# Turning both quantised activations by DMA in a fused attention and FP4 feed-forward kernel

## The reference

```python
x = layernorm(x + attn(x, W_write, W_read, decay, log_alpha))
x = layernorm(x + ffn(x, w_gate, w_up, w_down))

def fp4_quant_dequant(x):            # blocks of 16 along the last dimension
    scale = max(max(abs(xb)) / 6.0, 1e-12)
    xn = xb / scale
    q = GRID[searchsorted(MID, abs(xn))] * sign(xn) * scale   # GRID 0, .5, 1, 1.5, 2, 3, 4, 6
def fp4_linear(x, w):
    return einsum('bsk,nk->bsn', fp4_quant_dequant(x), fp4_quant_dequant(w))
gate = fp4_linear(x, w_gate)         # 256 -> 704
y = fp4_linear(x, w_up)              # 256 -> 704
h = silu(gate) * y
return fp4_linear(h, w_down)         # 704 -> 256
```

## Time and profile before

| | |
|---|---|
| time, median of 3 runs | 324.39 us (324.23 to 324.56) |
| span of the profiled execution | 322.5 us |
| TensorE busy | 314.5 us (97%) |
| VectorE busy | 293.0 us (91%) |
| GpSimd busy | 238.2 us (74%) |
| ScalarE busy | 213.2 us (66%) |
| DMA queue of SP | 15.01 MB, 14.0% of 16 engines |

### The profile page before, as it was taken

One profiled execution on the slowest core, in us unless ns is written; L12 is line 12 of the kernel. 1 busy time (PEld: TensorE's weight loads), 2 busy tenths in 40 slices (PEclk: granted clock), 3 DMA queues, 4 the chain that ended last, 5 costly groups with the idle time before them and its releaser, 6 DMA issues.

```text
span 322.5 us, 6519 instructions
## 1 busy us (share of the span) xinstructions
PE 314.5 (97%) x2067; PEld 285.2 (88%) x2067; DVE 293.0 (91%) x746; ACT 213.2 (66%) x521; POOL 238.2 (74%) x258
## 2 busy tenths in 40 slices
PE   7999999999999999999999999999999999999994
PEld 3999988989998998999989998898989889998983
DVE  4799789989899999899998999889999999999973
ACT  7769994767775647844784556766675555665664
POOL 1999898668696868676886768777779588368872
PEclk9999999999999999999999999999999999999999
DMA  6830301010010200320020200021000000001002
GB/s 227 302 125 9 132 0 67 1 66 2 1 67 16 84 16 0 100 82 3 16 83 17 83 17 3 33 65 35 1 18 17 16 18 17 19 16 35 17 33 84
DMA packets 8242, 15.69 MB, mean 49 GB/s; under 512 B 1040, under 2 KB 5136, under 8 KB 8208
## 3 DMA queue, kind: packets, MB, share of 16 engines
q1 hardware_dynamic: 7920, 15.01, 14.0%
q10 hardware_dynamic: 288, 0.26, 0.3%
HBM read 11.08 MB, written 4.19 MB: 47 GB/s over the span
## 4 chain that ended last, share of the span: by engine, by line
PE 69%; DVE 17%; issue 5%; ACT 4%; POOL 3%; ACTq 0%; DVEq 0%; POOLq 0%
PE gu L1712 11%; PE gu L1716 11%; PE gu L1713 11%; PE bank L1817 5%; PE bank L1712 4%; PE bank L1716 4%; PE bank L1713 4%; PE bank L1722 3%; DVE h_y L1094 3%; PE bank L1725 3%; PE bank L1726 3%; DVE w_raw L1209 2%; DVE hqT_lo L1236 2%; DVE h_am L1215 2%; PE bank L1783 2%
## 5 line engine op out<-in xcount | busy, mean ns | idle before, releaser
L413 POOL TENSOR_TENSOR h_q<-h_g,h_ns 128x704 f32<-128x704 f32 x32 | 51.2, 1604 | 47.7 <-DVE h_g L1099 47.6
L1712 PE MATMUL gu<-guT_hi,xqT_hi 128*128 128x512 f32 (+1 forms) x192 | 74.0, 386 | 0.7 <-DVE w_raw L1209 0.6
L1713 PE MATMUL gu<-guT_lo,xqT_hi 128*128 128x512 f32 (+1 forms) x192 | 72.2, 376 | 0.0
L1716 PE MATMUL gu<-guT_hi,xqT_lo 128*128 128x512 f32 (+1 forms) x192 | 56.6, 376 | 0.0
L699 ACT ACTIVATE w_raw<-gu 128x512 f32<-128x512 f32 x64 | 29.3, 462 | 32.7 <-PE gu L1716 32.4
L406 POOL TENSOR_TENSOR h_n<-w_raw,h_rs 128x704 f32<-128x704 f32 x32 | 47.0, 1472 | 3.4 <-DVE h_rs L1089 3.2
L719 ACT CAST hqT_hi<-bank 128x512 fp32r<-128x512 f32 x64 | 30.4, 478 | 17.7 <-PE bank L1817 17.2
L1712 PEld LDWEIGHTS gu<-guT_hi,xqT_hi 128*128 128x128 f32 x192 | 36.1, 188 | 6.0 <-ACT xqT_hi L688 0.9
L1716 PEld LDWEIGHTS gu<-guT_hi,xqT_lo 128*128 128x128 f32 x192 | 35.5, 188 | 6.0 <-ACT xqT_lo L693 0.2
L1713 PEld LDWEIGHTS gu<-guT_lo,xqT_hi 128*128 128x128 f32 x192 | 36.1, 188 | 4.8
L1094 DVE SCALAR_TENSOR_TENSOR h_y<-h_sq,h_n 128x704 f32<-128x704 bf16 x34 | 36.9, 1090 | 0.0
(11 more groups left out here) (159 smaller groups left out, 936.7 us busy)
## 6 DMA issues: line engine op xcount, KB each, us to landing
xs<-in_x_rows_dram SPq DMA_DIRECT2D x8, 512.0 KB, 3.4
out_dram<-wq_gu SPq DMA_DIRECT2D x32, 128.0 KB, 1.7
x_full<-in_xt_rows_dram SPq DMA_DIRECT2D x7, 512.0 KB, 3.2
w_raw<-in_w_ffn_dram SPq DMA_DIRECT2D x6, 352.0 KB, 6.0
w_pair<-in_w_attn_dram SPq DMA_DIRECT2D x1, 512.0 KB, 5.2
x_full<-in_xt_rows_dram SPq DMA_DIRECT2D x1, 256.0 KB, 2.6
x_full<-in_xt_rows_dram ACTq DMA_DIRECT2D x1, 256.0 KB, 3.4
scal<-in_scalars_dram ACTq DMA_DIRECT2D x1, 1.0 KB, 1.7
```

The source lines that it names most:

```text
L413: nc.gpsimd.tensor_tensor(blocks(h_q[:, p, 0:I]), blocks(h_g[:, p, :]), per_block(h_ns[:, p, :], HB), ALU.mult).then_inc(h_quant, 1)
L1712: nc.tensor.matmul(dst, lh, rh, start=(first and i == 0), stop=False)
L1713: nc.tensor.matmul(dst, lh, rl, start=False, stop=False)
L1716: last = nc.tensor.matmul(dst, ll, rh, start=False, stop=(end and i == len(terms) - 1))
```

## The change

For tiles 0 to 29 and for all x, TensorE no longer transposes activations. What is on the grid (x_g, h_g) becomes bf16, which holds its values exactly, and a DMA on SP transposes it (turn_x_grid, turn_h_grid) from SBUF to SBUF. The scales take another way: they are written in the order of the chunks into x_ns or h_ns, TensorE transposes them (one lone transpose per tile or half batch, x_scale_rows, h_scale_rows), ScalarE copies them to SBUF, SP writes them to DRAM and reads them back, each row 16 times (spread_x_scales, spread_h_scales). GpSimd multiplies the turned grid by the spread scales (x_spread, h_spread, now 768 wide), and ScalarE and VectorE split the product in one instruction each (h_round_all, h_rest_all), which read SBUF instead of PSUM. Tiles 30 and 31 keep the old way.

Beside it: all squares are written to PSUM in float32; the eight PSUM banks are one tensor with a place for every call given in tables; the subtractions of v and xq through the negated identity go; the negated mean of the output is folded into GpSimd's out_stats, except for the last tile; x_moments works on one column at a time; z_off shares the memory of dist. ScalarE issues the loads of x from batch 1 (rows) and 2 (transposed) on and all stores but the last; SP has the scale transfers and turns alone, behind the first loads. Before its first product gate_up waits for silu_ready, and for h_ready only before the second. All orders are new and written out without a loop. In TensorE's order gate_up(0) now stands ahead of reads(1, 1) and of everything of batch 2, down(4) behind gate_up(11), down(16) behind gate_up(23), down(24) behind gate_up(30, first half).

```diff
+        x_g = sb("x_g", [P, 2, PAIR], BF16)
+        x_gT = sb("x_gT", [P, 2, 2 * DK, P], BF16)
+        x_s = sb("x_s", [XHELD, 2, P])
+        x_sT = sb("x_sT", [P, 2, PAIR])
...
+        h_g = sb("h_g", [P, 2, HPAD], BF16)
+        h_gT = sb("h_gT", [P, 2, HC, P], BF16)
+        h_s = sb("h_s", [SHELD, 2, P])
+        h_sT = sb("h_sT", [P, 2, HPAD])
...
+        h_scales_dram = nc.dram_tensor("h_scales_dram", [B * TILES, SHELD, P], F32, kind="Internal").ap()
+        x_scales_dram = nc.dram_tensor("x_scales_dram", [2 * B, XHELD, P], F32, kind="Internal").ap()
...
+        def over_rows(rows, held, used):
+            return rows[0:KB * held, :].rearrange("(k c) t -> k (c t)", c=held)[:, 0:used * P].unsqueeze(1).to_broadcast((KB, BLK, used * P))
...
+            def write_h_scales(k, p, turn):
+                sp.wait_ge(hs_copied, k + 1)
+                sp.dma_start(h_scales_dram[k], h_s[:, p, :]).then_inc(hs_written[p], 16)
+            def spread_h_scales(k, p, turn):
+                sp.wait_ge(hs_written[p], 16 * turn)
+                if turn > 1:
+                    sp.wait_ge(h_quant, k - 1)
+                sp.dma_start(h_sT[:, p, :], over_rows(h_scales_dram[k], SC, HC)).then_inc(hs_landed[p], 16)
+            def turn_h_grid(k, p, turn):
+                sp.wait_ge(hg_repeated, k + 1)
+                if turn > 1:
+                    sp.wait_ge(h_quant, k - 1)
+                sp.dma_start_transpose(h_gT[:, p, :, :], h_g[:, p, :]).then_inc(hg_turned[p], 16)
...
+            write_h_scales(19, 1, 10)
+            spread_x_scales(6, 0)
+            spread_h_scales(19, 1, 10)
+            turn_h_grid(19, 1, 10)
+            write_h_scales(20, 0, 11)
+            turn_x_grid(6, 0)
+            turn_h_grid(20, 0, 11)
+            spread_h_scales(20, 0, 11)
...
+            def h_spread(k, p, turn):
+                pool.wait_ge(hs_landed[p], 16 * turn)
+                pool.wait_ge(hg_turned[p], 16 * turn)
+                if k >= 2:
+                    pool.wait_ge(hT_lo_ready, 2 * k - 2)
+                else:
+                    pool.wait_ge(wT_filled, FILLS)
+                nc.gpsimd.tensor_tensor(h_q[:, p, :], h_gT[:, p, :, :].rearrange("p c t -> p (c t)"), h_sT[:, p, :],
+                                        ALU.mult).then_inc(h_quant, 1)
...
-            def h_squares(k, p):
+            def h_squares(k, p, free):
                 act.wait_ge(h_norm, k + 1)
-                nc.scalar.activation(h_sq[:, p, :], h_n[:, p, :], ACT.Square, scale=ROOT_K).then_inc(h_square, 1)
+                wait_all(free)
+                nc.scalar.activation(two_banks(h_sq_at[k]), halves(h_n[:, p, :]), ACT.Square,
+                                     scale=ROOT_K).then_inc(h_square, 1)
...
+            def hg_repeat(k, p):
+                act.wait_ge(h_grid, k + 1)
+                nc.scalar.copy(h_g[:, p, I:HPAD], h_g[:, p, I - TAIL:I]).then_inc(hg_repeated, 1)
+            def repeat_h_scales(k, p):
+                act.wait_ge(h_div, k + 1)
+                ns = h_ns[:, p, 0:SROWS].rearrange("p (s e c) -> p c s e", s=2, c=SC)
+                nc.scalar.copy(ns[:, HC - 1, 1, :], ns[:, HC - 1, 0, :]).then_inc(hs_repeated, 1)
+            def copy_h_scales(k, p, turn):
+                act.wait_ge(hs_filled, k + 1)
+                if turn > 1:
+                    act.wait_ge(hs_written[p], 16 * turn - 16)
+                nc.scalar.copy(h_s[:, p, :], ps[0:SHELD, hs_at[k], 0:P]).then_inc(hs_copied, 1)
+            def h_round_all(k, p):
+                if k >= 2:
+                    act.wait_ge(down_filled, k - 1)
+                act.wait_ge(h_quant, k + 1)
+                nc.scalar.copy(hqT_hi[:, p, :], h_q[:, p, :]).then_inc(hT_hi_ready, 2)
...
+            def load_x_transposed(n):
+                act.wait_ge(xT_lo_ready, 2 * n)
+                act.dma_start(x_full[:].rearrange("p c t -> p (c t)"), xt_rows[n]).then_inc(xt_loaded, 16)
+            def store(k, slot):
+                act.wait_ge(out_ready, k + 1)
+                act.dma_start(out_rows[k], o_out[:, slot, :]).then_inc(stored[slot], 16)
...
+            def h_rest_all(k, p):
+                dve.wait_ge(hT_hi_ready, 2 * k + 2)
+                nc.vector.tensor_tensor(hqT_lo[:, p, :], h_q[:, p, :], hqT_hi[:, p, :].bitcast(F32),
+                                        ALU.subtract).then_inc(hT_lo_ready, 2)
...
+            def h_scale_rows(k, p, free):
+                pe.wait_ge(hs_repeated, k + 1)
+                wait_all(free)
+                nc.tensor.transpose(ps[0:SHELD, hs_at[k], 0:P], h_ns[:, p, :], ident[:]).then_inc(hs_filled, 1)
...
                 if k >= 1:
-                    pe.wait_ge(h_ready, 2 * k + half - 1)
+                    pe.wait_ge(h_ready if half else silu_ready, 2 * k + half - 1)
+                wait_all(free)
...
+                    if k >= 1 and m == 1:
+                        pe.wait_ge(h_ready, 2 * k - 1)
```

More of the change, by code:

```diff
@@ L1976, in _ @@
-            run(body)
-            down(12, 0, [(v_lo_ready, 13)])
-            values(6, 1, [(hT_lo_ready, 27)])
-            h_transpose(14, 2, 0, [(o_ready, 13)])
-            xq_transpose(4, 1, [(pr_ready, 27)])
+            h_scale_rows(3, 1, [(hs_copied, 3)])
+            reads(2, 1, [(wT_lo_ready, 8)])
+            x_scale_rows(2, 0, [(h_grid, 4)])
+            h_scale_rows(4, 0, [(h_grid, 4)])
+            gate_up(5, 1, 1, 1)
+            scores(3, 0, [(z_ready, 6)])
+            gate_up(6, 1, 2, 0)
@@ new lines, in _ @@
+            gate_up(8, 2, 0, 0)
+            down(1, 1, [(hs_copied, 7)])
+            scores(3, 2, [(v_lo_ready, 8)])
+            gate_up(8, 2, 0, 1)
+            scores(3, 3, [(pr_ready, 15)])
+            x_scale_rows(3, 0, [(o_ready, 2)])
+            h_scale_rows(7, 1, [(o_ready, 1)])
+            gate_up(9, 2, 1, 0)
+            reads(3, 1, [(h_grid, 8)])
+            gate_up(9, 2, 1, 1)
+            down(2, 2, [(z_ready, 8)])
+            down(3, 3, [(x_grid, 7)])
+            h_scale_rows(8, 0, [(pr_ready, 16)])
@@ new lines, in _ @@
+            gate_up(10, 2, 2, 0)
+            scores(4, 0, [(hs_copied, 9)])
+            scores(4, 1, [(h_grid, 9)])
+            values(4, 0, [(h_grid, 9)])
+            h_scale_rows(9, 1, [(pr_ready, 18)])
+            gate_up(10, 2, 2, 1)
+            gate_up(11, 2, 3, 0)
+            reads(4, 0, [(o_ready, 4)])
+            x_scale_rows(3, 1, [(pr_ready, 17)])
+            gate_up(11, 2, 3, 1)
+            down(4, 0, [(xs_copied, 8)])
+            down(5, 1, [(x_grid, 8)])
+            h_scale_rows(10, 0, [(z_ready, 9)])
@@ new lines, in _ @@
+            gate_up(12, 3, 0, 0)
+            values(4, 1, [(h_grid, 11)])
+            scores(4, 2, [(h_grid, 11)])
+            scores(4, 3, [(hs_copied, 11)])
+            h_scale_rows(11, 1, [(o_ready, 5)])
+            gate_up(12, 3, 0, 1)
+            gate_up(13, 3, 1, 0)
+            x_scale_rows(4, 0, [(hs_copied, 12)])
+            down(6, 2, [(pr_ready, 19)])
+            gate_up(13, 3, 1, 1)
+            reads(4, 1, [(h_grid, 12)])
+            down(7, 3, [(x_grid, 9)])
+            h_scale_rows(12, 0, [(z_ready, 10)])
@@ new lines, in _ @@
+            gate_up(14, 3, 2, 0)
+            scores(5, 0, [(o_ready, 7)])
+            scores(5, 1, [(o_ready, 8)])
+            values(5, 0, [(hs_copied, 13)])
+            h_scale_rows(13, 1, [(h_grid, 14)])
+            gate_up(14, 3, 2, 1)
+            gate_up(15, 3, 3, 0)
+            x_scale_rows(4, 1, [(hs_copied, 14)])
+            down(8, 0, [(pr_ready, 22)])
+            reads(5, 0, [(xs_copied, 10)])
+            gate_up(15, 3, 3, 1)
+            down(9, 1, [(o_ready, 9)])
+            gate_up(16, 4, 0, 0)
@@ L1982, in _ @@
+            values(5, 1, [(o_ready, 10)])
+            scores(5, 2, [(h_grid, 15)])
+            scores(5, 3, [(h_grid, 15)])
+            x_scale_rows(5, 0, [(z_ready, 11)])
+            h_scale_rows(14, 0, [(x_grid, 10)])
+            gate_up(16, 4, 0, 1)
+            gate_up(17, 4, 1, 0)
+            reads(5, 1, [(hs_copied, 15)])
+            scores(6, 0, [(h_grid, 16)])
+            h_scale_rows(15, 1, [(z_ready, 12)])
             gate_up(17, 4, 1, 1)
             gate_up(18, 4, 2, 0)
-            down(13, 1, [(pr_ready, 28)])
+            values(6, 0, [(xs_copied, 11)])
```

2554 lines of the change are left out of this document (1495 added, 1059 removed).

## The result

The changed kernel takes 334.37 us, the median of four runs (331.22 to 340.36), where the kernel before took 324.44 beside it: 1.027 times as long, 95% interval 1.025 to 1.030. Each median here is over all runs, while a ratio and its interval leave out disturbed runs, more than 1.5% above the fastest of their kernel (here 340.36). The prediction was 309, faster. The profiled execution took 333.26 us, its span is 331.5, and by the sum of the prediction it should have been 307.

What follows compares the result with a forecast made beforehand. TensorE was taken as the bound, VectorE 4% behind. TensorE's span of 322.5 less 22 is 300.5, plus 6 idle 306.5; with VectorE at 298 to 307, span 307 and median 309; forecast 303 to 314, full range 299 to 342.

Steps and rivals of the forecast that it cites:

- the one on the spread's engines: Spread of scales: 2.8 us, or 4.5 if 8 outer parts use half the engines; taken at 4, said not to matter.
- stands still for the landing of each write: SP waits 1.7 us for each write of scales to land, 78 us in all, within 265 us of tiles.
- 22 us less: TensorE's net saving: 28.3 us removed, 6.4 added for 46 lone scale transposes; 16 to 23 by the bounds.
- front gap: Start of TensorE's order, gate_up(0) waiting for a turn of x: 6 us idle charged, 0 to 12.
- 278 predicted: VectorE's busy time after 15 us less, 9 to 22; with idle time its span is 298 to 307.
- 138 issues at 0.33: SP's issues of scale writes, spreads and turns, 46 us; with 78 for landings, 124 us of some 265.
- The bound of 3.4 for a turn's issue: SP would bind only if issuing a turn took over 3.4 us, filling the 265 us in which tiles flow.
- turns bind: Rival: non-overlapping turns bind above 6.5 us per h turn; 340 us at 7; slower, chance 0.28.
- Its signs: Turns over 6.5 us would show as GpSimd's DMA waits ahead of its new product and TensorE below 90% mid-run.
- The block by block reading: Turn of h: 1309 ns per 128x128 block adds up, six make 7.9 us, time 375; 0.1 of the 0.28.
- Late but not binding: Rival: in-order engines lose part of the gain to late landings, front gap 12; 314 to 323 us, chance 0.15.
- pieces of one row each: Upper end for a 128x768 turn: 768 pieces of 256 bytes at 91 ns over 16 engines, 6.1 us with landing.

Runs made afterwards that it cites:

- the kernel with 8 parts: The changed kernel as it stands, its spreads reading 8 rows 16 times each; 334.37 us.
- the pair with and without the wait: Changed kernel with spreads reading 8 rows of an input (wrong values): 337.10 us waiting for the write's landing, 321.14 us not waiting.
- the pair in full computation: Changed kernel with scales held and written twice: spread reading 16 rows 8 times 319.29 us, only the first copy, 8 rows 16 times, 334.67 us.
- the pair that reads an input: Changed kernel with spreads reading an input, all waits kept (wrong values): 16 rows 8 times 315.00 us, 8 rows 16 times 337.10 us.
- neither transfer: Changed kernel without scale writes and spreads and without turns behind the first of each of four buffers (wrong values); 313.71 us, 0.967 of the kernel before.
- 16 parts and the new list: Changed kernel with scales held and written twice, spreads reading 16 rows 8 times, and SP's calls reordered; 315.69 us, 0.973 of the kernel before.
- turns alone: Changed kernel without the scales' writes and spreads (constant loads instead, wrong values), all turns kept; 314.19 us, 0.967 of the kernel before.
- the kernel with 16 parts: Changed kernel with scales held and written twice, spreads reading 16 rows 8 times, full computation; 319.29 us, 0.983 of the kernel before.
- trips of 8 parts without turns: Changed kernel without the turns behind the first of each of four buffers (wrong values), scale writes and spreads kept; 316.72 us, 0.974 of the kernel before.

## Why the prediction was wrong

**The step that failed** is the one on the spread's engines: "either value leaves the sum alone, since the scales run beside normalise, squares and grid." I had asked whether the spread's own landing (2.8 or 4.5 us) is hidden, and with 16 parts (4.0) it costs little. I had not asked what its packets do to the transfers behind and beside it. In the kernel with 8 parts a turn lands in 5.0 instead of 3.8 us and a write in 3.1 and 3.8 instead of 2.3 and 1.8. The term "stands still for the landing of each write" failed with it: I counted it as room on SP's list, 78 us in 265, and not as a delay that everything behind it takes over, which is worth some 16 us by the pair with and without the wait. That the delays of one tile reach the next through the written orders of the engines is my reading of the chain. The value of 8 parts against 16 is 15.4 us by the pair in full computation and 22, with the clock's share, by the pair that reads an input, of the 25 by which the time missed 309. The time of 334.4 lies inside the range of 299 to 342 by luck: its upper part was there for turns that bind, and they don't. The Trainium skill (DMA: Bandwidth & Descriptors, section "Why a DMA increments its semaphore by 16 and not by 1") states that the number of engines is the largest up to 16 that divides the slowest dimension of both sides; it was cited and dismissed. The runs agree with it: only the count of outer parts had to change, and the packets of a spread are in flight 8 at a time with 8 parts and 16 with 16. Which engines these are the traces don't tell.

The rest follows the order of the prediction.

TensorE: 22 us less was predicted. With neither transfer it is 314.5 - 294.7 = 19.8, within the 16 to 23; the lone transposes take 0.271 each from start to end, as the row said. Idle time was put at 8 + 6 = 14 us and is 312.3 - 294.7 = 17.6 there. The front gap is real: between 20 and 40 us TensorE is busy 16.14, and 15.71 with neither transfer, so 4 us where 6 were charged. But its two longest waits, 1.7 and 1.4 us, are put down to ScalarE's guT_lo and not to a turn, and they stand in both kernels; the reason given for it isn't shown. In the changed kernel itself both terms are off, 15.4 saved and 32.4 idle; with 16 parts and the new list they are 314.5 - 294.4 = 20.1 and 313.1 - 294.4 = 18.7 again.

VectorE: 278 predicted, 281.9 measured. h_y at 878 and h_g at 879 ns are the 886 and 870 taken, x_y at 684 the 692. The two subtractions out of SBUF lie at 1017 and 947 ns, against 929 and 681 without contention: 30 x 0.088 + 16 x 0.266 = 6.9 us, where 6.4 was taken. What was missed are small ones, such as h_ns with its scattered write (253 ns for 185).

ScalarE: its busy time rose by 12.4, and its issues, not counted as busy, are 31 x 0.34 + 13 x 0.33 = 14.8: 27 against 33. GpSimd's new product takes 1.784 us against 1.75. Neither binds.

SP: the term was 138 issues at 0.33, 46 us. They take 0.50 or 0.34 for a write, 0.61 for a spread and 1.23 for a turn: 30 x 2.34 + 16 x 2.18 = 105. The landings of the writes were 78 and are 59.4, so 164 us in place of 124, in 265. The bound of 3.4 for a turn's issue was not reached; SP is not full, it is late.

The turn: taken at 4 between 2.1 and 6.1; 2.8 us alone, 5.0 in the changed kernel. So the rival "turns bind" (T over 6.5) is out by the median, though single turns took up to 11.5, and turns alone at 314.19 show it. Its signs didn't show either: TensorE is at 95% in the middle, and of GpSimd's waits ahead of its new product 3.3 us are put down to a DMA, a spread. The block by block reading of the Trainium skill's price (VectorE: DVE Perf Modes, section "The three transpose paths"), 7.9 us and 375 in all (its own terms, 40.7 x 7.9 + 55, give 377), is out too: 2.8. "Late but not binding", 314 to 323, describes the kernel with 16 parts, 319.3. The changed kernel is that rival grown past its bound: no engine is busy over 91% of the span, and yet all wait. That case I had not listed.

The clock: I wrote that no part could be lost there, since it stood at 1.00 throughout. In the kernel before TensorE was idle 8.0 us in all; in the changed one it waited 4.4 us from 311.4 on, and from 310 to 320 the granted clock is 0.71. How much of the 20.7 us is this was not separated, but it is small: the changed kernel's busy time is 299.1 - 294.7 = 4.4 above the one with neither transfer for the same 1863 matmuls, and the one with turns alone had a mean of 0.982, no better than 0.984, and took 314.

Open is why the wait for the write costs as much as 16 us with 8 parts (337.1 against 321.1), when with 16 parts the wait and all else together cost 1.3 (315.0 against 313.7): landings are shorter there, but the delays were not followed tile by tile. Open is also why trips of 8 parts without turns cost only 3 us.

## What to carry to other kernels

A transfer that is hidden itself is not free: ask which DMA engines it fills, and what small transfer, on which a queue stands in order, shares them. When a broadcast is built, give it 16 outer parts rather than 8, even if the source must be written twice; here that was worth 15 us, and other numbers were not tried. And look for a change's cost by taking its transfers away one at a time and both together; here the one cost nothing, the other 3 us and both 21, which no sum of parts can give.

## What the runs showed of the hardware that I had not expected

A turning DMA takes SP 1.19 to 1.25 us to issue (medians), two to four times a plain one (0.34 to 0.61), in every kernel here that keeps all its turns. It moves many small pieces: the kernel with turns has 34,864 - 4,848 = 30,016 packets more on the queue for 42 turns, some 715 each, at 0.194 x 312.4 x 16 less 0.063 x 312.3 x 16 = 655 us of engine time, 22 ns each, where the kernel before had 91 for a packet. By the packet records 28,672 of them are of 256 bytes, 28 x 768 + 14 x 512, so the prediction's pieces of one row each are right, and its 91 ns as the price of a small one was four times too high. With 22 ns its own sum gives 768 x 0.022 / 16 = 1.1, and 1.7 to land, 2.8 us: what a turn of h takes with turns alone.

For the spreads with 8 outer parts the DMA section gives no time to landing, for those with 16 it does. That blank was a sign to be read: with 8 parts such a transfer is seldom named as what ended a wait (3.3 us, three times, ahead of h_q in the changed kernel), and 13.7 us of GpSimd's idle time ahead of x_q stand under "issue".
